# Experts: results stored by tile and collected by 64 indirect gathers, with a deeper loop order

## What is computed

```python
scores = sigmoid(x @ gate_w.T)                    # 1024 tokens, 64 experts in 8 groups
tidx = top 8 experts of a token, from its best 4 groups
tw = scores[tidx] / sum(scores[tidx]) * 2.5
for each token: x += sum over its 8 experts e of
    tw[e] * (silu(h @ We_gate[e]) * (h @ We_up[e])) @ We_down[e]     # 256 -> 128 -> 256
x += shared expert (same form)
```

## Time and profile before

| | |
|---|---|
| timed runs | 973.48, 974.66, 976.91 us, median 974.66 |
| profiled execution | 967.33 us, of which the span of the trace is 965.5 us |
| TensorE busy | 751.2 us (78%), mean granted clock 0.859 |
| VectorE busy | 464.4 us (48%) |
| ScalarE busy | 259.9 us (27%) |
| GpSimd busy | 271.1 us (28%), of which 2 x 79.4 us are gathers and scatters |
| DMA | 200.40 MB, mean 208 GB/s |

### The profile page before, as it was taken

How to read it: one execution, slowest core, us unless ns; L and a number is a source line. 1 busy time by engine, 2 the same in 40 slices (tenths; PEclk the granted TensorE clock), 3 DMA queues, 4 the chain that set the end, 5 groups by cost and what they waited for, 6 DMA issues and landing times. The chain is left out here.

```text
span 965.5 us, 19279 instructions
## 1 busy us (share of the span) xinstructions
PE 751.2 (78%) x6571; PEld 494.0 (51%) x6571; DVE 464.4 (48%) x1279; ACT 259.9 (27%) x520; POOL 271.1 (28%) x306
## 2 busy tenths in 40 slices
PE   5799999776659989889987789655667767665646
PEld 4455656455444546465447677534445545542315
DVE  4423335766736222233665886887523323222216
ACT  1121213744612211122454411341111111111150
POOL 1020002002502100000043551315566565564420
PEclk9999999988869999997995558977987887788878
DMA  8999991100985999911983200107666666568868
GB/s 331 383 372 380 417 404 62 51 1 2 332 286 221 352 390 408 396 61 31 193 189 87 69 5 1 44 1 238 194 200 194 192 197 191 186 184 260 262 213 322
DMA packets 70781, 200.40 MB, mean 208 GB/s; under 512 B 11912, under 2 KB 37744, under 8 KB 64944
## 3 DMA queue, kind: packets, MB, share of 16 engines
q1 hardware_dynamic: 60720, 176.29, 53.0%
q0 software_dynamic: 7680, 20.98, 6.9%
q10 hardware_dynamic: 2304, 2.10, 0.7%
HBM read 185.51 MB, written 13.83 MB: 206 GB/s over the span
## 5 line engine op out<-in xcount | busy, mean ns | idle before, releaser
L1989 PE MATMUL ps<-moe_wset,moe_xgT 128*128 128x256 f32 (+1 forms) x320 | 106.1, 464 | 57.2 <-DVE moe_xgT L2080 22.1
L2123 POOL DMA_INDIRECT moe_xg<-xn_rows,moe_idx x80 | 79.4, 992 | 106.1 <-DVE moe_idx L2071 68.4
L1989 PEld LDWEIGHTS ps<-moe_wset,moe_xgT 128*128 128x128 f32 (+1 forms) x320 | 62.9, 219 | 75.2 <-issue 48.2
L2132 POOL DMA_INDIRECT y_rows<-moe_ysb,moe_row x80 | 79.4, 993 | 35.9 <-issue 24.1
L2085 DVE TENSOR_TENSOR moe_hrow<-moe_hs,ps 128x128 f32<-128x128 f32 x80 | 22.9, 286 | 105.7 <-ACT moe_hs L2107 66.8
L2107 ACT ACTIVATE moe_hs<-ps 128x128 f32<-128x128 f32 x80 | 22.3, 278 | 174.3 <-PE ps L1989 86.3
L1469 POOL TENSOR_TENSOR ss_dec<-ss_dec,ss_cT 128x256 f32<-128x256 f32 x48 | 39.9, 869 | 93.5 <-ACT ss_dec L1424 51.0
L2080 DVE COPY moe_xgT<-ps 128x256 f32<-128x256 f32 x80 | 33.9, 424 | 63.4 <-remote 38.9
L2004 PE MATMUL ps<-moe_wset,moe_hT 128*128 128x256 f32 (+1 forms) x160 | 58.4, 453 | 2.4 <-DVE moe_hT L2090 1.6
L1282 PE MATMUL ps<-xnT,w_win 128*128 128x512 f32 x128 | 58.3, 614 | 0.0
L1314 PE MATMUL ps<-ss_dec 64*64 64x32 f32 (+2 forms) x1792 | 46.5, 255 | 11.5 <-issue 9.6
(11 more groups left out here) (401 smaller groups left out, 1412.3 us busy)
## 6 DMA issues: line engine op xcount, KB each, us to landing
x0ctxT<-ctx_T SPq DMA_DIRECT2D x8, 3202.0 KB, 19.2
x1ctxT<-ctx_T SPq DMA_DIRECT2D x8, 3202.0 KB, 13.8
x0ctxN<-ctx SPq DMA_DIRECT2D x8, 3072.0 KB
x1ctxN<-ctx SPq DMA_DIRECT2D x8, 3072.0 KB
moe_wset<-moe_gate_up SPq DMA_DIRECT2D x80, 256.0 KB
moe_wset<-L_ffn_We_down SPq DMA_DIRECT2D x80, 128.0 KB
moe_yg<-y_rows SPq DMA_DIRECT2D x7, 1024.0 KB, 11.0
ss_dec<-seg_rows SPq DMA_DIRECT2D x8, 768.0 KB, 17.0
```

The source lines that it names most:

```text
L1989: mm = pe.matmul(ps[c * n_:(c + 1) * n_, 2 + a2, 0:2 * FE], xgT[:, a2, h, c * n_:(c + 1) * n_], src[:, aw, h, :], start=h == 0, stop=h == ...
L2123: nc.gpsimd.indirect_dma_start(out=xg[:, a4, :], out_offset=None, in_=xn_rows, in_offset=bass.IndirectOffsetOnAxis(ap=idx[:, a4:a4 + 1], a ...
L2132: nc.gpsimd.indirect_dma_start(out=y_rows, out_offset=bass.IndirectOffsetOnAxis(ap=row[:, a4:a4 + 1], axis=0), in_=ysb[:, a4, :], in_offse ...
```

## The change

Results are no longer scattered. ScalarE's queue stores the 128 rows of a tile as one block to `y_rows`, whose row is now the slot. `rowt` and `row` go, and `marked` loses its order half; in its place TensorE makes three more products that give the bits of the token tile (160 matmuls of 104 columns in all), and VectorE puts the token together in four operations. SyncE first fills tiles 40 to 103 of `y_rows` with 8 DMAs of 1 MB. The collection is 64 indirect gathers on GpSimd, each of 128 rows of 1 KB, for a token tile and a choice k, by the slots in `sloti`. The choice weights are computed there, not in the tile loop, and VectorE alone does the weighted sum. In the loop TensorE's step becomes transpose n, gate/up n-2, transpose hidden n-4, down n-6, VectorE's `idx` n, `xgT` n-6, `hT` n-10, `hrow` n-8; there are 8 buffers of `xg`, `idx`, `ysb` and 4 of `xgT`, `silu`, `hrow`, `hidT` (two banks of PSUM each, as before).

```diff
 @block.sync
     sp.dma_start(xn_rows.rearrange("(j p) d -> p j d", p=P), xn[:]).then_inc(s_rows, 16)
+    for first in range(LEAST_TILES, MOST_TILES, NT):
+        sp.dma_start(y_rows[first * P:(first + NT) * P, :].rearrange("(j p) d -> p j d", p=P), xn[:]).then_inc(s_spare, 16)
...
 # index product, TensorE
-    mm = pe.matmul(ps[:, 4, 0:2 * MOST_TILES], in_tile[...], marked[...], ...)
+    mm = pe.matmul(ps[:, 4, 0:MOST_TILES], in_tile[...], marked[...], ...)
+    for x in range(3):
+        if j >> x & 1:
+            mm = pe.matmul(ps[:, 5 + x, 0:MOST_TILES], in_tile[...], of_tile[...], ...)
...
-PE step: transposes n, gate_up n-1, turn_hidden n-2, down n-3
+GU, TURN, DOWN, AHEAD = 2, 4, 6, 6
...
 # VectorE
 nc.vector.tensor_scalar(idx[:, m:m + 1], idxt[:, ds(n, 1)], 0, None, ALU.add).then_inc(s_ic, 1)
+copy to xgT of n-6:  dve.wait_ge(s_xt, k + 1); wait(dve, s_gu, k - 3)
+copy to hidT of n-10: dve.wait_ge(s_hx, k + 1); wait(dve, s_dn, k - 3)
+hrow of n-8:         dve.wait_ge(s_si, k + 1); wait(dve, s_hx, k - 3)
-row[:, a4:a4 + 1] <- rowt, after dve.wait_ge(s_ys[a4], ...)
-choice_weights(), weight_third(i)
...
 # ScalarE
+if live(DOWN + 1):
+    act.wait_ge(s_yc, k + 1)
+    act.dma_start(y_rows[ds(k * P, P), :], ysb[:, a8, :]).then_inc(s_ys[a8], 16)
+act.wait_ge(s_spare, (MOST_TILES - LEAST_TILES) // NT * 16)      # once, ahead of the loop
...
 # GpSimd
-nc.gpsimd.indirect_dma_start(out=y_rows, out_offset=bass.IndirectOffsetOnAxis(ap=row[:, a4:a4 + 1], axis=0), in_=ysb[:, a4, :], ...)
+for m in range(RING):                                            # once, behind the loop
+    pool.wait_ge(s_ys[m], rounds * 16)
...
 # collection
-SyncE: plain reads of y_rows into yg; TensorE: matmuls with diag; ScalarE: diag
+for j in range(NT):
+    for k in range(8):
+        nc.gpsimd.indirect_dma_start(out=yg[:, j, k * D:(k + 1) * D], out_offset=None, in_=y_rows[0:MOST_TILES * P, :],
+                                     in_offset=bass.IndirectOffsetOnAxis(ap=sloti[:, 0, j, k:k + 1], axis=0)
+                                     ).then_inc(collected(j, k), 16)
+VectorE: choice_weights(), 24 x weight_third(i), then 64 x
+    nc.vector.scalar_tensor_tensor(xt[:, j, :], y[:, k, :], w8[:, j, k:k + 1], xt[:, j, :], ALU.mult, ALU.add)
```

More of the change, by code:

```diff
@@ L1893, in _ @@
+                    nc.vector.tensor_copy(home[:], token)
+                    for x, plane in enumerate((ones_, twos)):
                         dve.drain()
[L1894 to L1897, removed]
+                        nc.vector.scalar_tensor_tensor(home[:], plane, float(P << x), home[:], ALU.mult, ALU.add)
@@ L1898, in _ @@
                     dve.drain()
[L1899 to L1910, removed]
+                    nc.vector.scalar_tensor_tensor(idxt[:, 0:MOST_TILES], fours, float(4 * P), home[:], ALU.mult, ALU.add)
@@ L2036, in _ @@
                     total = first + second
-                    gate_up(total * RING, 0, total, second)
-                    for r in range(2):
-                        turn_hidden(total * RING + r, r)
+                    for r in range(DOWN):
+                        if r < GU:
+                            gate_up(total * RING + r, r, total, second)
+                        if r < TURN:
+                            turn_hidden(total * RING + r, r)
                         down(total * RING + r, r, total, second)
-                    down(total * RING + 2, 2, total, second)
@@ L2066, in step @@
                     def step(n, m, g, live):
                         if live(0):
-                            k, (a4, a2) = n, slots(m, 0)
-                            if not early(k):
-                                dve.wait_ge(s_ga[a4], turn_of(g, m, 0) * 16)
-                            nc.vector.tensor_scalar(idx[:, a4:a4 + 1], idxt[:, ds(k, 1)], 0, None, ALU.add).then_inc(s_ic, 1)
-                        if isinstance(n, int) and n == 3:
-                            choice_weights()
-                            for i in range(2):
-                                weight_third(i)
@@ L2086, in step @@
-                        if live(5):
-                            k, (a4, a2) = n - 5, slots(m, 5)
-                            dve.wait_ge(s_hx, k + 1)
-                            wait(dve, s_dn, k - 1)
-                            nc.vector.tensor_copy(hT[:, a2, :], ps[:, 6 + a2, 0:P]).then_inc(s_hc, 1)
-                        if live(6):
-                            k, (a4, a2) = n - 6, slots(m, 6)
-                            if not early(k):
-                                dve.wait_ge(s_ys[a4], turn_of(g, m, 6) * 16)
-                            nc.vector.tensor_scalar(row[:, a4:a4 + 1], rowt[:, ds(k, 1)], 0, None, ALU.add).then_inc(s_rw, 1)
@@ L2096, in step @@
-                        if isinstance(n, int) and 4 <= n < 15:
-                            for i in (2 * n - 6, 2 * n - 5):
-                                weight_third(i)
-                    run(dve, step, 6)
+                            if not early(n):
+                                dve.wait_ge(s_ga[m], g * 16)
+                            nc.vector.tensor_scalar(idx[:, m:m + 1], idxt[:, ds(n, 1)], 0, None, ALU.add).then_inc(s_ic, 1)
+                        lag = AHEAD
+                        if live(lag):
+                            k, a4, b = n - lag, (m - lag) % 4, (m - lag) % 2
+                            dve.wait_ge(s_xt, k + 1)
+                            wait(dve, s_gu, k - 3)
+                            nc.vector.tensor_copy(xgT[:, a4, :, :], ps[:, b, 0:D].rearrange("p (h t) -> p h t", h=DH)).then_inc(s_xc, 1)
@@ L2100, in _ @@
+                    run(dve, step, AHEAD + TURN)
                 @block.scalar
@@ L2118, in step @@
                         if live(0):
-                            a4, a2 = slots(m, 0)
                             ready = nc.gpsimd.to_reg(n + 1)
```

247 lines of the change are left out of this document (107 added, 140 removed).

## The result

The changed kernel took 943.13 us (median of 4 runs, 941.23 to 951.0) against 974.07 us (4 runs, 968.52 to 976.91) for the one before: a ratio of 0.970, 95% interval 0.964 to 0.977. It is **31 us faster**; the prediction was 987, slower.

The account below looks back on a forecast made before the run. Nothing is full; between stops GpSimd sets the loop's pace, not TensorE. Index tables +2, tile loop -47 and collection +57 sum to +12 us on the profiled 967.3, giving 987 us from the median 974.66; range 957 to 1012.

Parts of the forecast that it names:

- The collection, +57: After the last result store: 64 gathers at 1.27 us pace the end, 91.2 us for 34.3; +57, bounds +38 and +62.
- Rival 2: Collection: gathers run without the 0.30 gap, so it costs +38, net -7, 968 us; chance 0.10.
- The index tables, +2: Stage before the loop: TensorE's 160 matmuls pace it, spare-row fill hidden; about +2 us, bounds -1 to +8.
- Rival 4: Index path: spare fill or matmuls cost more than hidden, +8, 995 us; counted within the likeliest case, no separate chance.
- The tile loop, -47: Loop over 80 tiles: whole tiles -41 and half tiles -6 make -47 us, bounds 0 to -81.
- The value of 2.6 us a tile: Whole tiles of the loop: TensorE's step plus what still shows of the stops, 2.6 us against 3.24 now, -41 us.
- ScalarE's stops as one in eight: Loop: ScalarE stops up to 6.8 us in one of eight tiles, 3 to 4 us showing, 0.4 us a tile.
- the -71 of the lower bound: Whole tiles of the loop at the DMA's floor of 2.13 us a tile: -71 us.
- a value of 3.7: Half tiles, the last 16: 3.7 us each against 4.08 now, DMA floor 3.43; -6 us, 0 to -10.
- rival 1: Loop reaches the DMA floor through the deeper order's slack: 2.2 us a tile, net -17, 958 us; chance 0.21.
- a DMA share of 0.9 in the loop: Sign in the profile after that the prediction is wrong on the fast side; it expected 0.75 to 0.8.
- Rival 3: Loop: stops grow with ScalarE's added instructions, the pace stays near 3.1 us a tile, net +48, 1023 us; chance 0.12.

Follow-up runs that it names:

- experiment 1: Changed kernel with the loop order of before (1, 2, 3 steps behind, index copies 3 ahead), deep buffers kept: 941.84 us, ratio 0.967 to the kernel before.
- experiment 4: Kernel before, own order and buffers, results stored by ScalarE instead of scattered, collection's plain reads kept, no putting in order: 887.97 us, ratio 0.911.
- experiment 3: Kernel before with only the deep order and deep buffers added, scatter and collection kept: 974.67 us, ratio 0.999.
- experiment 5: Kernel of experiment 4 with a second, unread gather of the same rows in each tile: 981.7 us, ratio 1.011 to the kernel before.
- experiment 2: Changed kernel, deep order, with GpSimd's indirect scatter in place of ScalarE's store: 1027.73 us, ratio 1.055 to the kernel before.
- experiment 8: Kernel of experiment 5 with the second gather cut to 16 rows of 1 KB: 980.14 us, ratio 1.011 to the kernel before.
- experiment 9: Kernel of experiment 5 with the second gather cut to 128 rows of 64 bytes: 979.5 us, ratio 1.004 to the kernel before.
- experiment 7: Kernel before with the gather replaced by a plain load of the first 128 tokens on SyncE, scatters kept: 980.16 us, ratio 1.009.
- experiment 10: Kernel of experiment 4 with a GpSimd memset and drain added in each tile, no second gather: 1032.61 us, ratio 1.058 to the kernel before.
- experiment 11: Kernel of experiment 5 with a memset and drain behind each of a tile's two gathers: 1347.67 us, ratio 1.382 to the kernel before.
- experiment 6: Kernel before with only odd tiles scattered, even ones stored by ScalarE into unread rows: two runs, 924.96 and 943.85 us, against 970.74.

## Why the prediction was wrong, step by step

**The collection, +57: right.** Measured +56.8 (91.1 us against a sum of 91.2). The gap of 0.30 is kept, the spacing is 1.30 for the 1.27 taken; the landing, block change and tail came as summed. The prediction's remark that the trace has no run of gathers without waits was wrong, for the four gathers from 653.45 to 657.83, at the start of the earlier trace rows, are one, at that same gap. Rival 2 is out. By the estimate from the Trainium skill ("DMA: Bandwidth & Descriptors", Anatomy of one DMA), 64 gathers without overlap were 147 us; the trace has 82.1, so the fixed part does overlap and the row was the better guide.

**The index tables, +2: within its bounds.** 44.8 us became 43.2 in the changed kernel and 44.8 again in experiment 1 (608.4 to 653.17), which has the same stage. The fill of spare rows is hidden, although the eight transfers take 11.0 us each to land (median) for the 4.4 taken: the last is issued at 620.7, 24 us before the weights start. Rival 4 is out.

**The tile loop, -47: the step that failed.** Measured -75.2. The value of 2.6 us a tile was built as TensorE's step plus what shows of the stops through a deeper order. Both ideas were wrong:
- The stops were carried over into the new kernel as if they were a fixed background of the loop. They belonged to the second indirect DMA of a tile, here the scatter that the change takes away; without it the loop is 87 us faster (experiment 4). The prediction took the scatter as 1.29 us of GpSimd's time and asked only who paces; that the stops might go with it was no rival and got no chance.
- Depth covers nothing of them (experiment 3: ratio 0.999), and where there are none it is not needed (experiment 1).

The stops were under-counted as well. The earlier trace rows has VectorE's row copy alone; the same view, 690 to 862, also has

```profile
ACT moe_hs L2107 <- remote: 43.1, 10, 7.3
ACT moe_ysb L2113 <- remote: 13.2, 5, 4.1
```

15 waits in some 53 tiles, where the prediction took ScalarE's stops as one in eight.

Without stops the tile sits at the DMA's floor: 2.07 against a computed 2.13, the -71 of the lower bound plus what a slightly better DMA rate gives (2.07 x 0.98 = 2.03 us busy). Half tiles: 3.76 for a value of 3.7. So **rival 1 came true in its place** (2.2 a tile, 958), and with it the sign that the prediction had named, a DMA share of 0.9 in the loop. But it did not come by its mechanism, which was slack from the deeper order. Its -67 - 9 for the loop stands beside the measured -75.2, of which the whole tiles alone are (3.24 - 2.07) x 64 = 75.

Of the 43 us between the forecast +12 and the measured -31, the loop is 28 and the index tables 4. The other 11 are no term of the prediction: they are the unchanged stretch and the distance of the two profiled executions from their medians, as said under the table. The rival's own sum, -17, is near the table's -20; of the 15 us between its 958 and the 943, the same 11 are most.

**Rival 3, stops that grow: out.** ScalarE has more instructions a tile than before, and one wait of 2.4 us left. Experiments 1 and 3 change the order and leave the stops as they are, gone or there. The instruction queues carry the same 48 and 29 packets in the profiles before and after, with stops and without, and in experiment 5 they carry none at all from 780 to 860, where six waits for "remote" stand. The Trainium skill ("Runtime: NRT & Kernel Launch", Instruction fetch mechanics) says that a taken branch outside the window forces a fetch; the trace shows no such fetch at these stops.

**Shown and not shown.** Shown: the stops, and with them the 84 to 94 us, come and go with a second indirect DMA on GpSimd in the loop (experiments 2, 4, 5, 8, 9), not with its direction, its rows or its bytes, and not with the order of the loop. With one scatter every 3.2 us (7) and with indirect DMAs 3.5 us or more apart (10, 11) there are none, but those loops are slower in everything else too. Whether GpSimd's occupation without indirect DMAs would do it wasn't settled (10).

Close spacing alone is not the condition. In the kernel before, 93 of 118 spacings from 660 to 860 are under 1.4 us, up to eight DMAs in a row. In experiment 6 they are 61 of 104, up to six in a row, with 10 waits for "remote" of over 1 us. In the changed kernel, from 660 to 780, they are still 10 of 60, up to four in a row, with the single wait of 2.4 us. So it takes more than a short burst; where the limit lies, in the length of the burst or in the mean rate, no run tells.

What a stop is, inside the chip, remains open, but the traces narrow it. All 28 waits for "remote" of the kernel before, from 660 to 860, stand at instructions that wait for a semaphore of TensorE. SyncE, whose weight loads wait for TensorE's down product, stands still with them:

```profile
729.26 0.07 SPq L2144 DMA_DIRECT2D moe_wset<-L_ffn_We_down  x1
729.34 0.60 PE L2004 MATMUL ps<-moe_wset,moe_hT 128*128 128x256 f32 x2
...
734.99 0.42 DVE L2080 COPY moe_xgT<-ps 128x256 f32<-128x256 f32 x1 [4.64 <-remote]
...
736.35 0.01 SPq L2142 DMA_DIRECT2D moe_wset<-moe_gate_up  x1
...
736.48 0.28 ACT L2107 ACTIVATE moe_hs<-ps 128x128 f32<-128x128 f32 x1 [5.28 <-remote]
```

The load at 736.35 needed the down product that the trace ends at 729.94. SyncE left pauses of 3.5 us or more between two load issues 13 times from 660 to 860; the changed kernel has none up to 780, the longest being 3.2. The fall of the DMA share with the stops fits this. So it is not a matter of VectorE or ScalarE alone. As the ends of matmuls are modelled in the profile, it can't tell whether TensorE's signals came late or TensorE itself did.

## What to carry to other kernels

An unexplained idle time is a term with an owner, not a background: before carrying it into the forecast, list what the change removes that could own it, and give a chance to its vanishing. When results must be permuted, the engine that writes them in the pipelined loop matters more than the length of a permutation at the end: here 57 us of exposed gathers bought 87 us. Where GpSimd issues two indirect DMAs for each step beside a busy loop, try to make one of them a plain store on another queue, before deepening any buffer.

## What the runs showed of the hardware that was not expected

- 16 indirect rows cost GpSimd 0.85 us and 128 rows 0.95: nearly all is a price per instruction, about 1.25 us with the 0.30 between two of them.
- Two indirect DMAs a tile in long bursts at 1.26 to 1.30 us spacing, beside matmuls and a stream of weights, stop VectorE, ScalarE and SyncE's loads for 2 to 9 us on about every fourth tile (9 to 16 times in some 60 tiles, 3 us or more lie between two starts of GpSimd). The DMA share falls to 0.64 to 0.67, or 0.75 where the second DMA is a full gather whose own bytes count (5); one a tile leaves it at 0.98.
- In the collection the same spacing of 1.30 us for 64 gathers stops no gather: all 63 gaps sum to 19.2 us, 0.30 each, and VectorE, busy 50 of 88 us, has no wait for "remote". There TensorE and ScalarE do no work.
- A drain behind a GpSimd memset of 0.96 us is followed by 1.7 to 2.0 us before the next gather, where gathers alone leave 0.30.
- TensorE's granted clock over the whole tiles is 1.00 in the changed kernel and in experiments 1 and 4, and 0.81 to 0.84 with the stops. Stops are not needed for a lower clock: with the fillers, where TensorE idles for other reasons, it is 0.87 (10) and 0.60 (11).
